# A graph network on one Trainium2 core: edge weights of the RGCN stored by its first layer and loaded by the other two, root products moved into the edge loops

## The reference, cut to what matters

```python
def _rgcn_layer(x, src, dst, edge_type, edge_attr, W, root, bias, nn_w, nn_b):
    edge_w = edge_attr @ nn_w.T + nn_b                 # (E, 32) @ (32, 256)
    msg = jax.nn.relu(x[src] * edge_w)                 # (E, 256)
    out = x @ root + bias
    for r in range(N_REL):                             # 3 edge types
        mask = edge_type == r
        s = jax.ops.segment_sum(jnp.where(mask[:, None], msg, 0.0), dst, num_segments=n)
        cnt = jax.ops.segment_sum(mask.astype(x.dtype), dst, num_segments=n)
        out = out + (s / jnp.maximum(cnt, 1.0)[:, None]) @ W[r]
    return out
for l in range(N_LAYERS):                              # 3 layers
    h = _rgcn_layer(h, src, dst, edge_type, edge_attr, W[l], root[l], bias[l], nn_w, nn_b)
```

## Time and profile before

| | |
|---|---|
| three runs | 5763.91, 5740.0, 5722.77 us; median 5740.0 |
| profiled execution | 5761.25 us, span 5759.5 us, granted clock 0.795 |
| busy share of the span | PE 67%, PEld 52%, DVE 51%, ACT 27%, POOL 52% |
| DMA over the span | 612.94 MB, mean 106 GB/s |
| RGCN layer 0: edge loop, node loop | 2856 to 3757, 3757 to 3855 us |
| layer 1 | 3855 to 4712, 4712 to 4804 us |
| layer 2 | 4804 to 5654, 5654 to 5744 us |

### The profile page before, as it was taken

The page is one execution under the profiler, slowest core; times in us unless marked ns, Lnnn a source line. Parts: engine busy times, 40 slices in busy tenths (PEclk is TensorE's granted clock), DMA queues, the critical chain, the costliest instruction groups (busy, mean ns, idle before and its releaser), DMA issues.

```text
span 5759.5 us, 109736 instructions
## 1 busy us (share of the span) xinstructions
PE 3862.1 (67%) x28772; PEld 2992.0 (52%) x28772; DVE 2909.8 (51%) x10493; ACT 1528.1 (27%) x3936; POOL 2987.9 (52%) x3069
## 2 busy tenths in 40 slices
PE   4122285766667766666588888886777777777768
PEld 1111143544444444444377777775666666666657
DVE  6444444555556555554644454544444454444446
ACT  0000004555552455555311111111111111111110
POOL 4666505555552455555455555525555644565561
PEclk7555587788888899888777777888887788877789
DMA  3111146666662566666322232213333322333331
GB/s 106 22 22 23 31 161 180 174 171 171 172 175 93 147 176 176 172 172 169 112 83 85 83 87 83 85 51 90 90 90 90 90 64 71 90 90 90 89 91 40
DMA packets 360700, 612.94 MB, mean 106 GB/s; under 512 B 119468, under 2 KB 233404, under 8 KB 358588
## 3 DMA queue, kind: packets, MB, share of 16 engines
q0 software_dynamic: 168960, 479.70, 29.7%
q1 hardware_dynamic: 132274, 117.26, 6.5%
q10 hardware_dynamic: 59402, 15.20, 1.1%
HBM read 560.06 MB, written 51.85 MB: 106 GB/s over the span
## 4 chain that ended last, share of the span: by engine, by line
PE 39%; another core or an unknown queue 20%; issue 15%; DVE 15%; DVEq 5%; ACT 3%; DMA 1%; ACTq 0%; POOL 0%; SPq 0%; POOLq 0%
PE bank L868 12%; PE bank L853 11%; PE bank L742 5%; DVEq L483 2%; DVE rings L1371 2%; DVE ht L1306 2%; PE bank L809 2%; ACT rings L936 2%; PE bank L819 2%; PE bank L782 2%; PE bank L792 1%; DVE ht L1293 1%; DVE region L1316 1%; DVE region L1390 1%
## 5 line engine op out<-in xcount | busy, mean ns | idle before, releaser
L427 POOL DMA_INDIRECT gring<-h_rows,gidx x1536 | 1506.0, 980 | 1075.0 <-DVE gidx L490 619.8
L868 PE MATMUL bank<-rings 128*128 128x96 f32 x6144 | 1110.5, 330 | 477.7 <-ACT rings L936 357.7
L868 PEld LDWEIGHTS bank<-rings 128*128 128x128 f32 x6144 | 1006.4, 238 | 605.5 <-DVE region L1390 392.5
L1371 DVE TENSOR_TENSOR rings<-bank,gring 128x512 f32<-128x512 f32 x768 | 529.9, 690 | 1237.3 <-PE bank L853 562.8
L936 ACT ACTIVATE rings<-rings 128x512 f32<-128x512 f32 x768 | 483.7, 630 | 2112.8 <-DVE rings L1371 1839.5
L853 PE MATMUL bank<-nnwt,rings 128*128 128x256 f32 x3072 | 1008.3, 460 | 9.1 <-DMA rings<-edge_attr_T 8.6
L427 POOL DMA_INDIRECT gring<-kv_rows,gidx x512 | 488.2, 953 | 614.3 <-issue 275.3
L809 PE MATMUL bank<-rings 128*64 128x128 f32 x4096 | 401.8, 325 | 512.1 <-ACT rings L966 236.5
L427 POOL DMA_INDIRECT ht<-kv_rows,gidx x512 | 489.4, 956 | 406.4 <-PE bank L835 202.1
L853 PEld LDWEIGHTS bank<-nnwt,rings 128*128 128x128 f32 x3072 | 647.5, 234 | 78.4 <-issue 9.0
L1390 DVE TENSOR_TENSOR region<-region,bank 128x192 f32 x1536 | 539.7, 351 | 95.5 <-DVE region L1390 1.1
(11 more groups left out here) (177 smaller groups left out, 4540.5 us busy)
## 6 DMA issues: line engine op xcount, KB each, us to landing
rings<-node_in_window_T SPq DMA_DIRECT2D x256, 128.0 KB
rings<-edge_attr_T SPq DMA_DIRECT2D x384, 64.0 KB
gring<-h_rows,gidx POOLq DMA_INDIRECT x1536
kv_rows<-rows SPq DMA_DIRECT2D x50, 258.0 KB, 2.3
edge_records<-gring SPq DMA_DIRECT2D x8, 1152.0 KB, 11.6
region<-edge_records SPq DMA_DIRECT2D x8, 1152.0 KB, 7.9
edge_attr_T<-gring ACTq DMA_DIRECT2D x32, 256.0 KB, 8.2
gring<-kv_rows,gidx POOLq DMA_INDIRECT x512
```

What stands on the lines that cost most here:

```text
L427: g.indirect_dma_start(out=slot_rows(i), out_offset=None, in_=rows, in_offset=bass.IndirectOffsetOnAxis(ap=gidx[:, quad, i % Q:i % Q + 1], ...
L868: ins = pe.matmul(b[:, (2 * k + c) * SEG:(2 * k + c + 1) * SEG], msg[:, slot % 2, (2 * k + c) * P:(2 * k + c + 1) * P], one, start=True, s ...
L1371: v.tensor_tensor(prod[:, slot % 2, :], bank[slot % RL][:, :], gring_r[:, 2 * slot:2 * slot + 2, :].rearrange("p k f -> p (k f)"), ALU.mul ...
```

## The change

The edge weights are made on PE in layer 0 alone. There, ACT copies each pair's 128x512 weights out of PSUM into SBUF (ewst, two places, the buffer of the node loop's rows), DVE's product reads that copy, and SP stores it to a new array in HBM (edge_weights, 256 KB a pair). In layers 1 and 2 PE makes no weights; SP loads them by pairs into four places (ER), each as soon as the product four pairs earlier is done. PE's weights of layer 0 now go to two banks and wait for ACT's copy (s_ewc), not for the product. ACT's relu lags by one pair (LAG_RELU).

The root products leave the node loops. In trips 0 to 24 of each edge loop, SP loads a block of h_rows (u = 0), PE transposes it (u = 2), ACT copies the transposes out, PE multiplies by root (u = 4, before the sums of that step) and DVE adds the bias into base (u = 6). The node loop keeps 12 records of PE and three instructions of DVE a block, the first of which reads base; the transposes and the copies to ht are gone from it, and from ahead of layer 0.

The diff, cut to its core:

```diff
+ER = 4
+def run_node_steps(eng, lag, step):
+
+    for u in range(U):
+        step(0, u, True)
+    with eng.Fori(1, NT) as trip:
+        for u in range(U):
+            step(trip, u, True)
+    with eng.Fori(NT, TRIPS) as trip:
+        for u in range(U):
+            step(trip, u, False)
+    for u in range(lag):
+        step(TRIPS, u, False)
...
+        ewst = rows[:, 0:4 * D].rearrange("p (s f) -> p s f", s=2)
+        hrow, hts = xr[:, 0, :], xr[:, 1, :].rearrange("p (c n) -> p c n", c=2)
+        base = ht_flat[:, :].rearrange("p (i f) -> p i f", f=D)
...
+        eat_flat = rings[:, 0:2 * Q * P].rearrange("p (s f) -> p s f", s=2)
+        def ew_slot(i):
+
+            return eat_flat[:, i, :] if i < 2 else ewst[:, i - 2, :]
...
-        LAG_SUM, LAG_RACC = 1, 2
+        LAG_RELU, LAG_SUM, LAG_RACC = 1, 1, 2
         ADDS = 2
-        STEPD = 4
+        STEPD = NREL
+
+        U_ROWS, U_ROOT, U_BASE = 2, 4, 6
...
-                def step(trip, u):
-                    if u % 2:
-                        return
+                def attributes(trip, u):
                     quad = u // 2
-                    wait_freed(sp, s_ew, l * PAIRS + trip * U + u - 2)
+                    wait_freed(sp, s_ew, trip * U + u - 2)
                     sp.dma_start(eat[0:ND, quad % 2, :, :],
                                  eat_d[bass.ds(trip, 1), :, quad * P:(quad + 1) * P]
                                  .rearrange("o (q j) e -> (o j) q e", q=Q)).then_inc(s_eat[quad % 2], 16)
 
+                def store_weights(trip, u):
+                    p, slot, r = tile_of(trip, u, 1)
+                    sp.wait_ge(s_ewc, p + 1)
+                    sp.dma_start(ew_d[bass.ds(p, 1), :, :].rearrange("o p f -> (o p) f"), ewst[:, slot % 2, :])\
+                        .then_inc(s_ewo[slot % 2], 16)
+
+                def load_weights(trip, u):
+                    p = trip * U + u
+                    wait_freed(sp, s_prod, l * PAIRS + p - ER + 1)
+                    sp.dma_start(ew_slot(u % ER), ew_d[bass.ds(p, 1), :, :].rearrange("o p f -> (o p) f"))\
+                        .then_inc(s_ewl[u % ER], 16)
+
+                def step(trip, u, nodes):
+                    if l == 0:
+                        if u % 2 == 0 and live(trip, u, 0):
+                            attributes(trip, u)
+                        if live(trip, u, 1):
+                            store_weights(trip, u)
+                    else:
+                        load_weights(trip, u)
+                    if nodes and u == 0:
+                        wait_freed(sp, s_htp, l * NT + trip)
+                        sp.dma_start(hrow, h_d[l][bass.ds(trip * P, P), :]).then_inc(s_hrow, 16)
+
                 if l == 0:
                     sp.wait_ge(s_clr, 3)
+                    sp.wait_ge(s_h, 16 * (NT // HG))
                     for i in range(EO):
                         sp.wait_ge(s_eato[i], 16 * 4 * NUC // EO)
-                run_steps(sp, 0, step)
+                else:
+                    for i in range(4):
+                        sp.wait_ge(s_ho[l - 1][i], 16 * len(range(i, NT, 4)))
+                    for i in range(2):
+                        sp.wait_ge(s_ewo[i], 16 * PAIRS // 2)
+                    sp.wait_ge(s_ew, PAIRS)
+                run_node_steps(sp, 1 if l == 0 else 0, step)
...
-            for i in range(NT):
-                pe.wait_ge(s_ln, i + 1)
-                features(pe, i, x1[:, i, :], i)
...
-                    for r in range(-1, NREL):
-                        o = bank[b + (r + 1) // 2][:, (r + 1) % 2 * D:((r + 1) % 2 + 1) * D]
+                    for r in range(NREL):
+                        o = bank[b + r // 2][:, r % 2 * D:(r % 2 + 1) * D]
                         for c in range(2):
-                            lhs = ht[:, c, i * P:(i + 1) * P] if r < 0 else \
-                                racc[:, c * NREL + r, i * P:(i + 1) * P]
-                            ins = pe.matmul(o, lhs, wts[:, l % 2, r if r >= 0 else NREL, c, :], start=c == 0, stop=c == 1)
+                            ins = pe.matmul(o, racc[:, c * NREL + r, i * P:(i + 1) * P], wts[:, l % 2, r, c, :],
+                                            start=c == 0, stop=c == 1)
                     ins.then_inc(s_dn, 1)
-                    if l < 2 and i:
-                        pe.wait_ge(s_dv, STEPD * n)
-                        features(pe, i - 1, orow[:, (i - 1) % 4, :], (l + 1) * NT + i - 1)
-                if l < 2:
-                    pe.wait_ge(s_dv, STEPD * (l + 1) * NT)
-                    features(pe, NT - 1, orow[:, (NT - 1) % 4, :], (l + 1) * NT + NT - 1)
...
         def relation_tiles(pe, l):
             at = l * PAIRS
 
-            def step(trip, u):
-                if live(trip, u, 0):
+            def step(trip, u, nodes):
+                if l == 0 and live(trip, u, 0):
                     p, slot, r = tile_of(trip, u, 0)
                     b = slot // 2 % 2
                     if slot % 2 == 0:
-                        pe.wait_ge(s_eat[b], 16 * (quads_before(l * TRIPS + r, slot) + 1))
-                    wait_freed(pe, s_prod, at + p - RL + 1)
+                        pe.wait_ge(s_eat[b], 16 * (quads_before(r, slot) + 1))
+                    wait_freed(pe, s_ewc, p - 1)
                     for k in range(2):
-                        ins = pe.matmul(bank[slot % RL][:, k * D:(k + 1) * D], eat[:, b, 2 * (slot % 2) + k, :], nnwt[:, :],
+                        ins = pe.matmul(bank[slot % 2][:, k * D:(k + 1) * D], eat[:, b, 2 * (slot % 2) + k, :], nnwt[:, :],
                                         start=True, stop=True)
                     ins.then_inc(s_ew, 1)
+                if nodes and u == U_ROWS:
+                    pe.wait_ge(s_hrow, 16 * (l * NT + trip + 1))
+                    wait_freed(pe, s_ht, l * NT + trip)
+                    for c in range(2):
+                        ins = pe.transpose(bank[2][:, c * P:(c + 1) * P], hrow[:, c * P:(c + 1) * P], ident[:, :])
+                    ins.then_inc(s_htp, 1)
+                if nodes and u == U_ROOT:
+                    pe.wait_ge(s_ht, l * NT + trip + 1)
+                    wait_freed(pe, s_base, l * NT + trip)
+                    for c in range(2):
+                        ins = pe.matmul(bank[3][:, 0:D], hts[:, c, :], wts[:, l % 2, NREL, c, :], start=c == 0, stop=c == 1)
+                    ins.then_inc(s_root, 1)
                 if live(trip, u, LAG_SUM):
...
-                def relation_step(trip, u):
-                    p, slot, r = tile_of(trip, u, 0)
-                    act.wait_ge(s_prod, l * PAIRS + p + 1)
-                    wait_freed(act, s_sp, l * PAIRS + p - 1)
-                    act.activation(msg[:, slot % 2, :], prod[:, slot % 2, :], ACT.Relu).then_inc(s_msg, 1)
-
-                run_steps(act, 0, relation_step)
-                if l < 2:
-                    for i in range(NT):
-                        copy_features(i, (l + 1) * NT + i)
+                def relation_step(trip, u, nodes):
+                    if l == 0 and live(trip, u, 0):
+                        p, slot, r = tile_of(trip, u, 0)
+                        act.wait_ge(s_ew, p + 1)
+                        if not isinstance(trip, int) or slot >= 2:
+                            act.wait_ge(s_ewo[slot % 2], 16 * (r * (U // 2) + slot // 2))
+                        act.copy(ewst[:, slot % 2, :], bank[slot % 2][:, :]).then_inc(s_ewc, 1)
+                    if live(trip, u, LAG_RELU):
+                        p, slot, r = tile_of(trip, u, LAG_RELU)
+                        act.wait_ge(s_prod, l * PAIRS + p + 1)
+                        wait_freed(act, s_sp, l * PAIRS + p - 1)
+                        act.activation(msg[:, slot % 2, :], prod[:, slot % 2, :], ACT.Relu).then_inc(s_msg, 1)
+                    if nodes and u == U_ROWS:
+                        n = l * NT + trip
+                        act.wait_ge(s_htp, n + 1)
+                        wait_freed(act, s_root, n)
+                        act.copy(hts[:, :, :], bank[2][:, 0:2 * P].rearrange("p (c n) -> p c n", c=2)).then_inc(s_ht, 1)
+
+                run_node_steps(act, LAG_RELU, relation_step)
...
-                        v.wait_ge(s_htp, (l + 1) * NT + i - 3)
                     o = orow[:, i % 4, :]
-                    v.tensor_tensor(o, bank[b][:, 0:D], bias_r[:, l, :], ALU.add).then_inc(s_dv, 1)
                     for r in range(NREL):
-                        p = bank[b + (r + 1) // 2][:, (r + 1) % 2 * D:((r + 1) % 2 + 1) * D]
-                        v.wait_ge(s_dv, STEPD * n + r + 1)
-                        v.scalar_tensor_tensor(o, p, inv_t[:, r, i:i + 1], o, ALU.mult, ALU.add).then_inc(s_dv, 1)
+                        p = bank[b + r // 2][:, r % 2 * D:(r % 2 + 1) * D]
+                        if r:
+                            v.wait_ge(s_dv, STEPD * n + r)
+                        v.scalar_tensor_tensor(o, p, inv_t[:, r, i:i + 1], o if r else base[:, i, :], ALU.mult, ALU.add)\
```

(12 more changed lines are left out.)

34 lines of the change are left out of this document (16 added, 18 removed).

## The result

The changed kernel takes 5980.27 us (5971.61 to 5999.81, 4 runs) against 5741.66 us before: ratio 1.0419, 95% interval 1.0373 to 1.0464. It is 4.2% slower; 5900 us had been forecast. The profiled execution took 5999.81 us (span 5998.0), 238.5 us over the span before.

A forecast was written before the change was run, and what follows sets the result against it. Node loops were taken as bound by PE, edge loops as full-rate gathers broken by pauses. 5761 + 379 - 145 - 76 = 5919, less 21 to the median: 5898, say 5900 us; own range 5770 to 6030, 8 in 10 5590 to 6130.

The forecast's parts named there:

- Layer 0's ring: Layer 0's edge loop: weights, copy, relu, sums run one after another; 3.8 or 5.8 us a pair by clock, +379 us.
- the 0.2 us added for root steps and late products: Layer 0's edge loop: allowance on the middle pace of 4.8 us, giving 5.0 us a pair, 1280 us.
- Node loops: Node loops of all three layers: without root records and transposes PE's block falls from 3.67 to 2.58 us, -76 us.
- Root steps: Edge loops: hidden in layers 1 and 2, at most 27 us a layer; 0.14 us a pair in layer 0.
- Loads: Layers 1 and 2: weight loads have over 7.5 us against a landing of 4.4 us, so they hide.
- the byte bound: Edge loops of layers 1 and 2: weights beside gathered rows limit the pace to 880 us, +26 a layer; range end only.
- Layers 1 and 2: Their edge loops: without PE's weights and short waits, 3.05 us a pair, 781 us each, -145 us together.
- A pause of 3.3 us for six pairs instead of for about four: Edge loops of layers 1 and 2: long waits keep their length but come later, giving 3.05 us a pair.
- Rival A: Edge loops of layers 1 and 2: long waits vanish, gathers' floor of 655 us reached, -397 us, kernel 5646 us; chance 0.22.
- B: Layer 0's edge loop: PE stays at 1.2 GHz, 6.0 us a pair, +635 us, kernel 6154 us; chance 0.12.
- C: Layer 0: PE stays at 2.4 GHz, +123 us; layers 1 and 2 reach the gathers' floor; kernel 5390 us; chance 0.09.
- The clock rule: PE in layer 0: gaps of 1.4 us at most never gate the clock; by it alone the kernel takes 5642 us.

The follow-up runs named there:

- e3_order: The changed kernel with ACT's relu of the previous pair moved ahead of the copy of edge weights; 5754.24 us, ratio 1.000 to the kernel before.
- e8_noroot: e3_order without load, transposes, product and bias of the root in the edge loops (output not the reference's); 5818.03 us, ratio 0.994 to the kernel before.
- e4_clock: The changed kernel plus two matmuls a pair that nobody reads in layers 1 and 2, where weights were made; 6071.26 us in one run.
- e9_gate7: e7_gate with POOL's gathers waiting for the sums of the pair eight before instead of six; 4469.54 us, ratio 1.0114 to the kernel before.
- e11_direct: e7_gate with layer 0's product reading weights in PSUM and the copy behind relu; 4625.71 us, ratio 1.0459 to the kernel before.
- e7_gate: e3_order plus POOL's gathers waiting for the sums of the pair six before, all RGCN layers; 5617.98 us, ratio 0.9586 to the kernel before.

## Why the prediction was right, and where it was off

- **Layer 0's ring**: right, mechanism and both prices (3.72 and 5.70 us against 3.8 and 5.8); e3_order took it away. The mean was 4.66 us a pair, not 5.0: +293 us, not +379. The clock was the guess in it, and it was 0.72: about as many steps at either level. The mean lies under even the middle of the two paces, 4.8, so the 0.2 us added for root steps and late products was too much.
- **Node loops**: -68 against -76 us; a block took 2.59 us, 2.58 forecast. The 11 us ahead of layer 0 were not in the sum.
- **Root steps**: forecast as hidden in layers 1 and 2 and 0.14 us a pair in layer 0, some 36 us. e8_noroot gives 0.6%, 35 us, over all three, with some 5 and 8 us in layers 1 and 2 when its loops (866, 866) are set beside e3_order's on another chip. That fits, but layer 0's part is not shown: its loop was no shorter without them (970 against 958).
- **Loads**: hidden, as argued, but for 15 to 25 us a layer. The loops' 860 and 871 us lie near the 880 of the byte bound by chance: without the loads they stay at 841 and 857.
- **Layers 1 and 2**: here a step failed. "A pause of 3.3 us for six pairs instead of for about four" assumed that the pauses hang on how far the product lags. Measured: 56 and 57 pauses in 256 pairs, one in 4.5, of 3.2 to 3.5 us, hence +24 and not -145 us. What held instead: a pause comes when signals of PE are held up for long enough, and they are held up as the gathers are issued, whoever makes the weights. The weights' absence was worth some 30 us a layer (e4_clock), loads and roots took most of that back, and the rest is within what two loops of one kernel differ by (860 and 871). The sum also took 3.3 us, one pause seen whole, where the mean of the 75 was 2.5, and 2.5 us a pair for the gathers beside its own floor of 2.56. The first slip makes its pace 0.14 us too long, the second 0.06 too short.
- **Rival A**, the gathers' floor, did not occur, for the reason that its text gave against it: the long waits did not end with PE's weights. On the quiet chip the floor is there before the change as well. **B and C**: the ring ran at both levels, between them.
- **The forecast's own range**: paces of 4.5 to 5.5 and 2.85 to 3.25 us a pair give 128 us and 102 us to either side, 5668 to 6128 and not 5770 to 6030.
- **The clock rule** of the Trainium skill ("TensorE: Matmul & The Clock Gate", Part 1: The HAM clock gate): taken strictly, the ring should never have fallen to the lower clock, and the trace does not agree. From 2876 to 4039 us PE's longest recorded gap is 1.95 us, and yet the granted clock averages 0.72 there; from 4003 to 4033 us it is 0.50, with gaps of about 1.3 us. In layers 1 and 2 the clock fell to 0.57, and getting it back (0.81) gained nothing.

+293 + 24 - 68 - 11 = 238 against +158 forecast. That the total came this near is in part luck: two errors met, 86 us too much in layer 0 and 169 us too much gain in layers 1 and 2.

## What to carry to other kernels

Before moving work onto an engine with time to spare, write down its program order beside those of the engines it answers to: one copy ahead of one relu made a ring of four steps and cost 4.2%, and swapping two blocks of code took all of it back. When a wait has no named end, look at what stops just before it ends, count how often that is so, and test it before costing any change in the loop. A producer that need not run at full depth can be made to stop early, on the slowest consumer's signal: 3.2% in the kernel before, 4.1% in the changed one with the order mended (ratio 0.9586, the fastest relative to before of all kernels that do the whole work), nothing lost on a quiet chip in the kernel before.

## What the runs showed of the hardware that was not expected

- On three of the four chips with a number on record the signals of PE's matmuls were late in the edge loops; in the one hold-up followed above they arrived 8.7 and 9.7 us after the record's end, while POOL issued indirect gathers 1.25 us apart. Without the gathers the waits were gone. About half of the long ones ended some 2 us after the gathers stopped, the others while they went on. They were absent where POOL ran about 4 gathers at a time (layer 0 of the changed kernel, but for its first 35 us); whether the length of the run decides it was not tested. Whether the signals or the matmuls themselves are late, the records (whose ends are modelled) can't tell. It does not hang on the gathers' bytes (117 against 161 GB/s), nor on PE's clock (0.57 or 0.81).
- TensorE's granted clock went between its two levels again and again in layer 0's edge loop (0.94 from 3500 to 3530, 0.50 from 4003 to 4033), though from 2876 on PE's longest recorded gap there was 1.95 us.
- On one chip the hold-up did not occur, and the same kernel took 4420 us there instead of 5740 to 5864. So one chip's ratio may not hold on another: e9_gate7 and e11_direct can't be set beside e7_gate.
